# Four-layer attention and FFN kernel: first loads and row filling of the softmax attentions issued in the projection block, units ordered by batch

## What is computed

```
L1:  q = x Wq + bq ; k, v from ctx (1024 rows) ; attn = sparsemax(q k^T / 4) ; (attn v) Wo + bo
L2:  src = norm(x) ; q, k, v from src (512 rows) ; attn = softmax(q k^T / 4) ; (attn v) Wo + bo
L3:  q = x Wq.T + bq ; k, v from ctx (1024 rows) ; logit = q k^T / 4 ; attn = softmax(logit) ; attn v
```

## Time and profile before

| | us |
|---|---|
| median of 3 runs (3883.28 to 3884.93) | 3883.99 |
| the profiled execution | 3882.62 |
| its span, first to last instruction | 3880.5 |
| PE busy | 2609.7 (67%) |
| DVE busy | 2520.9 (65%) |
| ACT busy | 1473.8 (38%) |
| POOL busy | 589.0 (15%) |
| end of m2p's units to first matmul of m2a | 2833.4 to 2853.0 |
| end of l3p's units to first matmul of l3a | 3342.0 to 3373.4 |

### The profile page before, as it was taken

One profiled execution on the slowest core, in us unless ns is written; L12 is line 12 of the kernel. 1 busy time (PEld: TensorE's weight loads), 2 busy tenths in 40 slices (PEclk: granted clock), 3 DMA queues, 4 the chain that ended last, 5 costly groups with the idle time before them and its releaser, 6 DMA issues. The chain is left out here.

```text
span 3880.5 us, 38725 instructions
## 1 busy us (share of the span) xinstructions
PE 2609.7 (67%) x11365; PEld 1661.5 (43%) x11366; DVE 2520.9 (65%) x4807; ACT 1473.8 (38%) x2226; POOL 589.0 (15%) x255
## 2 busy tenths in 40 slices
PE   2888887352433222334799994878778697699678
PEld 2443334230111111112688883555433586344367
DVE  4989885757777888774445552556555455566377
ACT  2444441214667667664222222222135122156321
POOL 0554453000000000000221210111110111200021
PEclk8999898575666566666899997899889798699889
DMA  1000000031000000000111101000041110522011
GB/s 56 13 12 9 13 8 18 16 140 44 22 23 1 22 22 22 22 1 32 49 41 49 49 8 46 1 0 0 8 135 46 33 43 19 183 50 61 18 37 35
DMA packets 46338, 136.43 MB, mean 35 GB/s; under 512 B 8568, under 2 KB 18816, under 8 KB 41600
## 3 DMA queue, kind: packets, MB, share of 16 engines
q1 hardware_dynamic: 46208, 135.01, 11.7%
HBM read 106.28 MB, written 28.31 MB: 35 GB/s over the span
## 5 line engine op out<-in xcount | busy, mean ns | idle before, releaser
L1373 ACT ACTIVATE l1a_over_s<-l1a_sc_s,l1a_ntau_s 128x1024 bf16<-128x1024 f32 x272 | 312.2, 1148 | 149.1 <-DVEq L1401 141.1
L1199 PE MATMUL ps<-ident,l1a_worst_s 128*1 128x128 f32 x8 | 3.0, 370 | 484.4 <-DVEq L1460 484.4
L1692 PE MATMUL ps<-m1e_x_part_s,m1e_up_part_s 128*128 128x512 f32 x1296 | 297.9, 391 | 22.0 <-POOL m1e_up_part_s L1788 15.9
L1254 DVE MAX8 l1a_cand_s<-ps 128x8 f32<-128x128 f32 x1024 | 218.6, 284 | 136.4 <-PE ps L1159 130.4
L1692 PEld LDWEIGHTS ps<-m1e_x_part_s,m1e_up_part_s 128*128 128x128 f32 x1296 | 243.8, 189 | 74.0 <-issue 23.7
L662 POOL TENSOR_TENSOR l0a_prob_sum_s<-l0a_prob_sum_s,l0a_probs_s 128x1024 f32<-128x1024 f32 x96 | 233.3, 2431 | 229.3 <-ACT l0a_probs_s L622 224.4
L622 ACT ACTIVATE l0a_probs_s<-l0a_clipped_s 128x1024 f32<-128x1024 f32 x128 | 135.5, 1058 | 308.6 <-DVE l0a_clipped_s L553 307.6
L1159 PE MATMUL ps<-l1a_ka_s,l1a_qa_s 128*128 128x512 f32 x256 | 146.4, 591 | 109.8 <-ACT l1a_sc_s L1325 89.6
L1325 ACT ACTIVATE l1a_sc_s<-ps 128x512 f32<-128x512 f32 x256 | 153.0, 598 | 171.8 <-DVE l1a_cand_s L1254 171.8
L1199 PEld LDWEIGHTS ps<-ident,l1a_worst_s 128*1 128x1 f32 x8 | 0.6, 79 | 491.2 <-issue 428.4
L948 DVE TENSOR_REDUCE l3a_shift_s<-ps 128x1 f32<-128x1024 f32 x128 | 151.3, 1220 | 86.9 <-PE ps L871 86.6
(11 more groups left out here) (516 smaller groups left out, 5978.3 us busy)
## 6 DMA issues: line engine op xcount, KB each, us to landing
m1ew_up_s<-m_up SPq DMA_DIRECT2D x9, 1536.0 KB, 6.5
l1a_ka_s<-l_k_parts SPq DMA_DIRECT2D x16, 512.0 KB, 7.7
l3a_ka_s<-l_k_parts SPq DMA_DIRECT2D x16, 512.0 KB, 8.2
m1ew_down_s<-m_down SPq DMA_DIRECT2D x9, 768.0 KB, 4.2
l0a_w_s<-l_w SPq DMA_DIRECT2D x16, 384.0 KB, 2.9
m3ew_up_s<-m_up SPq DMA_DIRECT2D x6, 768.0 KB, 4.1
l_v_groups<-l1p_v_all_s SPq DMA_DIRECT2D x2, 2048.0 KB, 7.1
l1a_qa_s<-l_q_parts SPq DMA_DIRECT2D x16, 256.0 KB, 5.9
```

What stands on the lines that cost most here:

```text
L1254: ins = nc.vector.max(T["cand"][:, r, 8 * (c + j * 4):8 * (c + j * 4) + 8], ps[:, f % 2, c * P:(c + 1) * P])
L1373: nc.scalar.activation(T["over"][:, :], T["sc"][:, r, :], ACT.Relu, bias=T["ntau"][:, r:r + 1], accum_out=T["total"][:, r:r + 1]).then_inc ...
L1692: ins = nc.tensor.matmul(ps[:, 2 * (u % 2) + way, :], up_parts[a][:, k, way, c, :], x_parts[b][:, k, half * BANK:(half + 1) * BANK], start ...
```

## The change

A class `HeadTiles` now owns `qa`, `ka`, `v`, the semaphore `filled`, and two sets of load semaphores, one for queries and keys (four DMAs, LOADS = 16 * 4) and one for values. `slots` makes it before `normalize` and frees it after `project_out`, for m2 and l3; l1 (sparse) gets none. `project_heads` takes it as an argument. There SP, behind the last unit's stores, waits for the stores of the first half of the units (those of batch 0) and issues the twelve query and key loads of groups 0 to 2, then the two v stores, and after these have landed the three v loads. POOL does the six fillings behind its work on `v_all` and waits for them. In `dense_attention` the loads and fillings at the start are gone, and PE waits for the values only before the first value product of a group. The order of units is batch, then half, then queries and keys, in l1p too. The groups 3 to 7 are loaded as before, with the same five DMAs.

```
+class HeadTiles:
+    BUFS, LOADS = 3, 16 * 4
...
+    def fill(self, pool):
+        for buf in range(self.BUFS):
+            pool.memset(self.qa[64:128, buf, :, :].bitcast(F32), 0.0).then_inc(self.filled, 1)
+            pool.memset(self.ka[64:128, buf, :, :].bitcast(F32), 1.0).then_inc(self.filled, 1)
+
+    def load_qk(self, sp, n):
+        buf = n % self.BUFS
+        for i in range(2):
+            sp.dma_start(self.qa[32 * i:32 * i + 32, buf, :, :].rearrange("r h n -> r (h n)").bitcast(F32),
+                         self.q_parts[i, n:n + 1].rearrange("o r h n -> (o r) (h n)").unsqueeze(1).to_broadcast(
+                             [16, 2, 4 * NQ])).then_inc(self.qk_loaded[buf], 16)
+            sp.dma_start(self.ka[32 * i:32 * i + 32, buf, :, :].rearrange("r h n -> r (h n)").bitcast(F32),
+                         self.k_parts[n:n + 1].rearrange("o r a h n -> (o r a) (h n)")
+                         ).then_inc(self.qk_loaded[buf], 16)
+
+    def load_v(self, sp, n):
+        buf = n % self.BUFS
+        sp.dma_start(self.v[:, buf, :, :, :].rearrange("p c h n -> p (c h n)"),
+                     self.v_groups[n:n + 1].rearrange("o p n -> (o p) n")).then_inc(self.v_loaded[buf], 16)
...
-        units = [(0, m, b, 0) for m in range(KC) for b in range(B)]
-        units += [(1, m, b, j) for m in range(KC) for b in range(B) for j in range(nk // BANK)]
+        units = [(what, m, b, j) for b in range(B) for m in range(KC)
+                 for what, j in [(0, 0)] + [(1, j) for j in range(nk // BANK)]]
...
                 sp.dma_start(dest(what, 1, m, b, j), lo[:, u % 3, :].bitcast(F32)).then_inc(lo_stored[u % 3], 16)
+            if tiles is not None:
+                for j in range(3):
+                    sp.wait_ge(hi_stored[j], 16 * len(range(j, U // 2, 3)))
+                    sp.wait_ge(lo_stored[j], 16 * len(range(j, U // 2, 3)))
+                for n in range(tiles.BUFS):
+                    tiles.load_qk(sp, n)
             for b in range(B):
                 sp.wait_ge(v_ready, (b + 1) * TV // B)
                 sp.dma_start(v_groups[4 * b:4 * b + 4].rearrange("g p n -> p g n"),
                              v_all[:, 4 * b:4 * b + 4, :, :, :].rearrange("p g c h n -> p g (c h n)")
                              ).then_inc(v_stored, 16)
             sp.wait_ge(v_stored, 32)
+            if tiles is not None:
+                for n in range(tiles.BUFS):
+                    tiles.load_v(sp, n)
...
             pool.memset(v_all[:, :, :, :, 16:17].rearrange("p g c h o -> p (g c) (h o)"), 1.0).then_inc(v_cleared, 1)
+            if tiles is not None:
+                pool.wait_ge(v_cleared, 2)
+                tiles.fill(pool)
+                pool.wait_ge(tiles.filled, 2 * tiles.BUFS)
...
-            load(0)
-            load(1)
-            load(2)
             place(0)
             for n in range(G - 1):
                 if 0 < n <= G - BUFS:
                     sp.wait_ge(pv_done, NC_ * n)
-                    load(n - 1 + BUFS)
+                    tiles.load_qk(sp, n - 1 + BUFS)
+                    tiles.load_v(sp, n - 1 + BUFS)
                 place(n + 1)
...
-            for buf in range(BUFS):
-                pool.memset(qa[64:128, buf, :, :].bitcast(F32), 0.0).then_inc(filled, 1)
-                pool.memset(ka[64:128, buf, :, :].bitcast(F32), 1.0).then_inc(filled, 1)
...
                 pe.wait_ge(exp_done, (n * NC_ + t) * S + S)
+                if t == 0:
+                    pe.wait_ge(v_loaded[n % BUFS], 16 * (n // BUFS + 1))
```

More of the change, by code:

```diff
@@ L665, in _, with __init__, project_heads @@
             over_groups(pool, lambda: None, step)
-def project_heads(nc, name, ps, x_t, kv_t, nk, w, bias, bv_dram, loaded, q_parts, k_parts, v_groups):
+class HeadTiles:
+    BUFS, LOADS = 3, 16 * 4
+    def __init__(self, nc, name, nk, q_parts, k_parts, v_groups, stack):
+        s = stack.enter_context(Stage(nc, name))
+        self.nk, self.q_parts, self.k_parts, self.v_groups = nk, q_parts, k_parts, v_groups
+        self.qa = s.sb("qa", [P, self.BUFS, 4, NQ], F32R)
+        self.ka = s.sb("ka", [P, self.BUFS, 4, nk], F32R)
+        self.v = s.sb("v", [P, self.BUFS, nk // P, 4, 32])
+        self.filled = s.sem("filled")
+        self.qk_loaded = [s.sem(f"qk_loaded{j}") for j in range(self.BUFS)]
+        self.v_loaded = [s.sem(f"v_loaded{j}") for j in range(self.BUFS)]
+    def fill(self, pool):
[15 more added lines that the diff above has]
+                     self.v_groups[n:n + 1].rearrange("o p n -> (o p) n")).then_inc(self.v_loaded[buf], 16)
+def project_heads(nc, name, ps, x_t, kv_t, nk, w, bias, bv_dram, loaded, q_parts, k_parts, v_groups, tiles=None):
     SCALE = 16 ** -0.5
@@ L774, in _, with dense_attention @@
             pool.memset(v_all[:, :, :, :, 16:17].rearrange("p g c h o -> p (g c) (h o)"), 1.0).then_inc(v_cleared, 1)
-def dense_attention(nc, name, ps, ident, slot_pick, spread, nk, q_parts, k_parts, v_groups, o_all):
-    G, S, BUFS = 8, 4, 3
+            if tiles is not None:
+                pool.wait_ge(v_cleared, 2)
+                tiles.fill(pool)
+                pool.wait_ge(tiles.filled, 2 * tiles.BUFS)
+def dense_attention(nc, name, ps, ident, slot_pick, spread, nk, tiles, o_all):
+    G, S, BUFS, LOADS = 8, 4, tiles.BUFS, tiles.LOADS
     NC_ = nk // P
@@ L789, in dense_attention @@
     TURN_AT = NC_ - 2
-    LOADS = 16 * 5
     HALVES = ((0, 6), (6, 8))
     with Stage(nc, name) as s:
-        qa = s.sb("qa", [P, BUFS, S, NQ], F32R)
-        ka = s.sb("ka", [P, BUFS, S, nk], F32R)
-        v = s.sb("v", [P, BUFS, NC_, S, 32])
+        qa, ka, v, filled = tiles.qa, tiles.ka, tiles.v, tiles.filled
+        qk_loaded, v_loaded = tiles.qk_loaded, tiles.v_loaded
         shift = s.sb("shift", [P, 2, ROWS])
@@ L800, in dense_attention @@
         rden_parts = s.sb("rden_parts", [P, NQ], F32R)
-        filled, zeroed = s.sem("filled"), s.sem("zeroed")
-        qk_loaded = [s.sem(f"qk_loaded{j}") for j in range(BUFS)]
+        zeroed = s.sem("zeroed")
         pair_made, pair_used = s.sem("pair_made"), s.sem("pair_used")
@@ L813, in _ @@
         def _(sp):
[L814 to L824, removed]
             def place(n):
@@ L2493, in slots @@
             v_groups = nc.dram_tensor(tag + "_v_groups", (8, P, nk), F32).ap()
+            held = ExitStack()
+            tiles = None if sparse else HeadTiles(nc, tag + "h", nk, q_parts, k_parts, v_groups, held)
             with ExitStack() as st:
@@ L2500, in slots @@
                 project_heads(nc, tag + "p", ps, x_t, x_t if kv_t is None else kv_t, nk, w, bias,
-                              A[tag + "_bv"], loaded, q_parts, k_parts, v_groups)
+                              A[tag + "_bv"], loaded, q_parts, k_parts, v_groups, tiles)
             with ExitStack() as st:
@@ L2507, in slots @@
                 else:
-                    dense_attention(nc, tag + "a", ps, ident, slot_pick, spread, nk, q_parts, k_parts, v_groups, o_all)
+                    dense_attention(nc, tag + "a", ps, ident, slot_pick, spread, nk, tiles, o_all)
                 project_out(nc, tag + "o", ps, o_all, 4, wo_dram, bo_dram, acc, by_batch=True)
+            held.close()
         if 0 in stages:
```

## The result

| | before | after |
|---|---|---|
| median of 5 runs each, us | 3883.28 (3879.98 to 3884.93) | 3907.95 (3901.28 to 3913.21) |
| profiled execution, us | 3882.62 | 3905.57 |
| m2p, block start to last lo store | 16.0 | 22.3 |
| last lo store of m2p to first matmul of m2a | 19.6 | 25.2 |
| m2a, first to last row maximum | 116.2 | 114.7 |

The account below looks back on a forecast made before the run. A chain of stages with barriers, whose DMA queue is served in order. Joins 5.2 + 6.2 and units 3.4 + 7.9 sum to +22.7 us, added to the median of 3884.0: 3906.7 us, range 3888 to 3918.

Parts of the forecast that it names:

- (a): Start of m2a and l3a: no wait for group 0 or the filling, -9.4 and -12.1 us at an unchanged block start.
- (b): End of m2p and l3p: twelve loads ahead of the v stores take 14.7 and 22.0 us, and the stores wait.
- rival of v stores that aren't held up: Joins: v stores land without waiting for the loads; -13.4 us, 3870.6, or about -4 with port waits; chance 0.17.
- loads at 375 GB/s: Loads before the v stores run at the stores' rate, taking 8.4 and 12.6 us; +7.0 us, 3891; chance 0.04.
- (d): Last lo store to first matmul: 24.8 against 19.6 us in m2 (+5.2), 37.7 against 31.5 in l3 (+6.2).
- (c): Three v loads issued behind the landed v stores: 1.4 us on SP before the barrier, their transfer costing nothing.
- (e): Units of m2p and l3p: CASTs take turns with POOL's filling memsets, last lo store +3.4 and +7.9 us later.
- the pace of the stores: Last units of l3p: storing 456 GB/s, over the queue's 375, may add 1 to 1.5 us; left to the range.
- POOL keeps the port: Units of m2p and l3p: CASTs begin after all six memsets, +7.9 and +11.2 us; total +30.5, 3914.5; chance 0.14.
- rule for who goes next: Shared port in m2p and l3p: memset and CAST alternate, a turn being both less some 0.15 us.
- (f): Units ordered by batch in all three attentions: cost 0, bounds -1 and +1 us; l1's only edit.
- Everything behind the first matmul unmoved: Sign expected in the changed profile: nothing after each attention's first matmul moves, nor does l1.

Follow-up runs that it names:

- e6: Changed kernel with fillings held until the last unit is done and the twelve query and key loads issued behind the v stores; 3873.06 us, ratio 0.9975.
- e2: Changed kernel with all loads back in the attention, leaving the early fillings and the unit order; 3896.16 us, ratio 1.0036 to the kernel before.
- e5: Changed kernel with POOL waiting for each filling to be done before starting the next; 3901.64 us, ratio 1.0055 to the kernel before.
- e9: The changed kernel measured again, unaltered; 3901.63 us, ratio 1.0057 to the kernel before.
- e1: Changed kernel with POOL's six fillings starting only when the last unit's low part is made; 3889.55 us, ratio 1.0017 to the kernel before.
- e8: Changed kernel with the six whole fillings done twice; 3914.67 us in one run.
- e7: Changed kernel with each filling cut into four memsets, one for each head; 3915.81 us in one run.
- e3: Kernel before with only the unit order changed to batch, half, queries and keys; 3883.69 us, ratio 1.0002.
- e4: Changed kernel with late fillings and only group 0's query and key loads ahead of the v stores, other loads in the attention; 3866.45 us, ratio 0.9955.

## Why the prediction was right, and where it was off

The direction, the size and both mechanisms held. By its own steps:

- *(a), (b)*: right. First matmuls 0.2 us behind the block's start; loads at 214 and 210 GB/s, v stores at 365 and 381. The stores queued behind the loads, with landings of 12.4 to 14.4 and 23.1 to 23.4 us. The Trainium skill (DMA: Bandwidth & Descriptors, Queues, rings and completion order) states that a DMA engine takes one ring's descriptors in order; with this the trace agrees, by those landings. The rival of v stores that aren't held up is refuted by the change and by e6, and that of loads at 375 GB/s by the windows. The clock stood at 0.50 before either first matmul, as before.
- *(d)*: m2 25.2 for 24.8, l3 39.2 for 37.7. The data kept to the sum: in windows of 0.4 us l3's loads began 2.2 us behind the last lo store, gave way to the v stores at about 24.0 and these fell off at about 35.4, where 2.0, 24.0 and 35.2 had been put. The terms that were too small stand behind them in l3: SP went on 1.7 us later, not 0.6, and from its last issue to the first matmul passed 0.8 us, not 0.5. In m2 the loads began at about 2.6 for 2.0. Sum +13.3 for +11.4.
- *(c)*: right, 1.29 us for the three v issues; no wait for the values is seen in either attention.
- *(e)*: +3.2 for +3.4 in m2 and +8.6 for +7.9 in l3 wherever all turns were taken (e2, e5, e9), and fillings of 10.5 to 12.5 us by medians for 11.3. In l3p the six turns took the time forecast; the last CASTs behind them came every 1.35 us, not 1.15, with DVE waiting for a lo store before each of the last four: the pace of the stores, which the prediction had kept for the range. The memset behind a CAST was 0.28 us longer, not 0.4. The rival "POOL keeps the port" had put units at +7.9 and +11.2; what happened in m2p of the first profile, +6.3, is it in part: two turns, then a lost row. That the step named a rule for who goes next was too much; it is what nearly all contests show, not all. That CASTs wait at all is shown by 0.43 us of the same ones in e1 beside 1.38 to 3.09 in e8. The Trainium skill (SBUF — State Buffer, Who interferes with whom) has the shared port locked for a whole instruction; with long memsets the trace agrees, each CAST ending some 0.3 us behind the one that it met, while e7's row of memsets shows a wait far beyond one.
- *(f)*: right, e3.
- "Everything behind the first matmul unmoved" was wrong by 1.5 us to the good side in m2a: the split of the values' wait had been priced only for group 0, where it also serves groups 3 to 7.

Together 13.3 + 11.8 - 1.5 = +23.6 with all turns taken; the profiled execution adds 3.1 for the lost one. The medians say +24.7 and, for the repeat, +20.4. So the mechanisms were right, but that the first median lies only 2.0 us from the forecast is in part luck: terms too small by 2.4 us stand beside 1.5 us that were overlooked on the other side, and the same kernel measured 4 us less the second time.

**Open.** What decides whether a waiting CAST gets the boundary: the lost one in m2p met its memset 0.98 us behind its start, as the one before it did (0.99). Of the 65 CASTs that met memsets of 1.8 or 3.5 us in after, e2, e5, e8 and e9, one lost its boundary; with memsets of 0.5 to 0.9 us two got in at once and two lost a whole row. And what makes executions of the same kernel differ, by 14 us in before and by up to 18 in e4 and e6; between profiles part of it is l1a.

## What to carry to other kernels

A load moved ahead of a barrier costs its transfer, as far as nothing else covers it, if the queue holds behind it a store that the barrier waits for. Load ahead only what the next stage's first instruction needs (here a third, which turned +10 us into -17), and issue the rest after the barrier; behind the stores, as in e6, it was better than ahead of them, but not as good. Work given to an idle POOL isn't free where DVE rounds from SBUF to SBUF: put it where DVE does something else (in e1 it stood beside the additions into `v_all`, which read PSUM and kept their 0.42 us), and don't count on small pieces to help: in the one run that had them they made it worse.

## What the runs showed of the hardware

- A waiting CAST is let in at a boundary between long memsets, though POOL has no gap there (64 of 65), but in e7 two CASTs lost every boundary of a row of short ones: 10.37 and 15.49 us for a CAST of 0.43.
- The one that is let in lengthens the next memset by 0.28 us in the record (1.80 to 2.08; 0.17 in e5, where POOL pauses between fillings), less than its own 0.43, and the CAST ends 0.29 us behind the recorded end of the one that it met, so it seems to start a little before that end.
- Loads onto 32 partitions took all of the queue's time at 210 to 214 GB/s, and the stores right behind them from 128 partitions 365 to 381, in the same queue and with the same share of engine time (0.96 to 1.02).
